# The pair loop of a fused attention and expert kernel written out, and its router steps put at other slots

## The reference, cut to what matters

```python
x = x + tanh(g_xattn) * xattn(layernorm(x), ctx, Wq, Wkv, Wfc, fc_b, qn_w, kn_w)   # 4 heads of 64
x = x + tanh(g_ffn) * ffn(layernorm(x), Wr, We)                                    # 8 experts, top 2

# xattn: q and k are RMS-normalised for each head
attn = softmax(einsum("bqhd,bkhd->bhqk", q, k) * 64 ** -0.5)
out = einsum("bhqk,bkhd->bqhd", attn, v) @ Wfc + fc_b

# ffn: the router
logits = einsum("btd,ed->bte", x, Wr)
top_vals, top_idx = top_k(logits, 2)
w = softmax(top_vals)
pos = cumsum(onehot(top_idx)) - onehot(top_idx)     # place of the token in its expert's queue
keep = pos < 97                                     # capacity of an expert in a batch
out = sum over the two experts e of a token:  w_e * (x @ We[e]) where keep, else 0
```

## Time and profile before

| what | value |
|---|---|
| median of 3 runs | 1496.6 us (1494.82 to 1496.76) |
| span of the profiled execution | 1506.5 us |
| busy share of the span: PE, DVE, ACT, POOL | 95%, 73%, 59%, 51% |
| PE busy, matmuls | 1433.3 us, 8320 |
| granted TensorE clock, mean | 0.983 |
| DMA | 28 GB/s, q14 instruction 81 packets |

### The profile page before, as it was taken

The page is one execution under the profiler, slowest core; times in us unless marked ns, Lnnn a source line. Parts: engine busy times, 40 slices in busy tenths (PEclk is TensorE's granted clock), DMA queues, the critical chain, the costliest instruction groups (busy, mean ns, idle before and its releaser), DMA issues. The chain is left out here.

```text
span 1506.5 us, 30216 instructions
## 1 busy us (share of the span) xinstructions
PE 1433.3 (95%) x8320; PEld 1194.0 (79%) x8320; DVE 1093.6 (73%) x3085; ACT 888.2 (59%) x2536; POOL 764.2 (51%) x915
## 2 busy tenths in 40 slices
PE   5899999999999999999999999999999999999998
PEld 4688887878788887887878878787888878878886
DVE  5667767777777677767778777777776777677763
ACT  6546656656566556566556566565566566666552
POOL 3335455445455445555545555444655554554454
PEclk8689999999999999999999999999999999999999
DMA  4000000000000000000000000000000000000000
GB/s 142 19 1 33 33 31 10 32 26 32 33 15 25 33 25 33 32 10 30 25 33 32 33 7 32 26 32 33 32 7 33 25 33 32 22 18 32 8 16 27
DMA packets 29021, 42.76 MB, mean 28 GB/s; under 512 B 4672, under 2 KB 12288, under 8 KB 28928
## 3 DMA queue, kind: packets, MB, share of 16 engines
q1 hardware_dynamic: 28928, 41.90, 8.1%
HBM read 25.11 MB, written 16.78 MB: 28 GB/s over the span
## 5 line engine op out<-in xcount | busy, mean ns | idle before, releaser
L305 PE MATMUL bkM<-we,x2T 128*128 128x512 f32 x3072 | 789.8, 399 | 1.1 <-DVE acc_v L933 1.1
L305 PEld LDWEIGHTS bkM<-we,x2T 128*128 128x128 f32 x3072 | 556.0, 189 | 110.6 <-DVE acc_v L933 1.8
L606 ACT ACTIVATE a_out<-bkM,gate 128x256 f32<-128x256 f32 x512 | 215.2, 475 | 187.4 <-PE bkM L305 185.1
L450 POOL TENSOR_TENSOR a_sum<-a_sum,a_out 128x256 f32<-128x256 f32 x256 | 188.4, 736 | 131.4 <-ACT a_out L606 112.7
L933 DVE SCALAR_TENSOR_TENSOR acc_v<-bkM,gate,acc_v 128x256 f32<-128x256 f32 x384 | 185.6, 483 | 36.8 <-PE bkM L305 27.0
L406 POOL TENSOR_TENSOR rstd<-ve,minus_half 128x4 f32<-128x4 f32 x64 | 64.8, 1012 | 256.6 <-DVE ve L740 256.6
L406 POOL TENSOR_TENSOR q_r<-q_ve,minus_half 128x16 f32<-128x16 f32 x32 | 93.2, 2911 | 135.0 <-DVE q_ve L816 135.0
L517 ACT ACTIVATE xn<-x_sb,shift,rstd 128x256 f32<-128x256 f32 x128 | 66.5, 590 | 111.8 <-DVE shift L749 111.8
L437 POOL TENSOR_TENSOR probs<-probs,p_inv 128x308 f32<-128x308 f32 x128 | 90.3, 716 | 79.1 <-DVE p_inv L831 79.1
L406 POOL TENSOR_TENSOR k_r<-k_ve,minus_half 77x8 f32<-77x8 f32 x32 | 52.3, 1633 | 122.1 <-DVE k_ve L789 122.1
L455 POOL TENSOR_TENSOR y<-a_sum,acc_v 128x256 f32<-128x256 f32 x128 | 94.0, 735 | 10.9
(11 more groups left out here) (162 smaller groups left out, 2799.1 us busy)
## 6 DMA issues: line engine op xcount, KB each, us to landing
x_sb<-in_x SPq DMA_DIRECT2D x32, 512.0 KB, 3.6
out<-y SPq DMA_DIRECT2D x64, 256.0 KB, 2.0
ctx_sb<-in_ctx SPq DMA_DIRECT2D x32, 154.0 KB
stage<-in_L_ffn_We SPq DMA_DIRECT2D x2, 1024.0 KB, 8.0
stage<-in_L_xattn_Wkv SPq DMA_DIRECT2D x1, 512.0 KB, 5.9
stage<-in_L_xattn_Wq SPq DMA_DIRECT2D x1, 256.0 KB, 6.2
stage<-in_L_xattn_Wfc SPq DMA_DIRECT2D x1, 256.0 KB, 4.1
bias_bc<-in_L_xattn_fc_b SPq DMA_DIRECT2D x1, 128.0 KB, 5.3
```

The source lines that it names most:

```text
L305: mm = nc.tensor.matmul(out, l, r, start=(i == 0), stop=(i == len(terms) - 1))
L450: nc.gpsimd.tensor_tensor(a, o[:, 0] if i == 1 else a, o[:, i], ALU.add).then_inc(a_summed.sem, 1)
L606: ins = nc.scalar.activation(a_out[:, t % 2, (e // 4) * 2 + i], bkM[1][:, i * D:(i + 1) * D], ACT.Copy, scale=gate[:, m.parity, t, e:e + 1])
```

## The change

The hardware loop goes: each engine's program is all 32 rounds in a row, with constant counts in its waits. Inside a round, these steps stand elsewhere:

```diff
-        LOOPS = (PAIRS - 4) // 2
...
+            def pair(n):
+                return Pair(0, n) if n < PAIRS else None
+
             fill()
-            step(Pair(0, 0), Pair(0, 1), Pair(0, 2), Pair(0, 3))
-            with engine.Fori(0, LOOPS) as j:
-                step(Pair(j, 1), Pair(j, 2), Pair(j, 3), Pair(j, 4))
-                step(Pair(j, 2), Pair(j, 3), Pair(j, 4), Pair(j, 5))
-            step(Pair(LOOPS, 1), Pair(LOOPS, 2), Pair(LOOPS, 3), None)
-            step(Pair(LOOPS, 2), Pair(LOOPS, 3), None, None)
-            step(Pair(LOOPS, 3), None, None, None)
+            for n in range(PAIRS):
+                step(pair(n), pair(n + 1), pair(n + 2), pair(n + 3))
```

ScalarE's slots (the move of `x2T_part` ahead of `q(f, 1)` in slot 7 is left out):

```diff
-                if k == 8 and f:
-                    k_part(f)
+                if k == 8:
+                    if f:
+                        k_part(f)
+                    if p:
+                        logits(p)
                 if k == 9:
-                    if p:
-                        logits(p)
                     if f:
                         exps(f, 0)
...
-                if k == 12 and f:
-                    exps(f, 3)
+                if k == 12:
+                    if f:
+                        exps(f, 3)
+                    if p:
+                        router_exp(p)
                 if k == 13:
                     if f:
                         pT_part(f, 0)
                         pT_part(f, 1)
-                    if p:
-                        router_exp(p)
```

VectorE's slots (here too `x2T_part` now stands ahead of `q(f, 1)` in slot 7):

```diff
-                if k == 9 and f:
-                    row_max(f, 0)
-                    row_max(f, 1)
-                    row_max(f, 2)
-                    row_max(f, 3)
-                if k == 10 and m:
-                    experts(m, k)
+                if k == 9:
+                    if f:
+                        row_max(f, 0)
+                    if p:
+                        route(p, 0)
+                    if f:
+                        row_max(f, 1)
+                        row_max(f, 2)
+                        inverse(f, 0)
+                if k == 10:
+                    if m:
+                        experts(m, k)
+                    if f:
+                        row_max(f, 3)
+                        inverse(f, 1)
                 if k == 11:
-                    if f:
-                        inverse(f, 0)
-                    if p:
-                        route(p, 0)
-                    if f:
-                        inverse(f, 1)
+                    if p:
+                        route(p, 1)
+                    if f:
                         inverse(f, 2)
                 if k == 12:
                     if m:
                         experts(m, k)
                     if f:
                         inverse(f, 3)
-                    if p:
-                        route(p, 1)
                 if k == 13 and f:
                     pT_part(f, 0)
                     pT_part(f, 1)
                 if k == 14:
+                    if p:
+                        gates(p)
                     if f:
                         pT_part(f, 2)
                         pT_part(f, 3)
-                    if p:
-                        gates(p)
                     if m:
                         experts(m, k)
```

More of the change, by code:

```diff
@@ L637, in slot @@
                         q(f, 0)
-                        q(f, 1)
                     if p:
@@ L641, in slot @@
                         x2T_part(p, 1)
+                    if f:
+                        q(f, 1)
                     if m:
                         experts(m, k)
-                if k == 8 and f:
-                    k_part(f)
-                if k == 9:
+                if k == 8:
+                    if f:
+                        k_part(f)
                     if p:
                         logits(p)
+                if k == 9:
                     if f:
@@ L987, in slot @@
                         experts(m, k)
-                if k == 9 and f:
-                    row_max(f, 0)
-                    row_max(f, 1)
-                    row_max(f, 2)
-                    row_max(f, 3)
-                if k == 10 and m:
-                    experts(m, k)
-                if k == 11:
+                if k == 9:
                     if f:
-                        inverse(f, 0)
+                        row_max(f, 0)
                     if p:
@@ L1000, in slot @@
                     if f:
+                        row_max(f, 1)
[6 more added lines that the diff above has]
+                        row_max(f, 3)
                         inverse(f, 1)
+                if k == 11:
+                    if p:
+                        route(p, 1)
+                    if f:
                         inverse(f, 2)
@@ L1199, in slot @@
                     kv(f, 1)
-                if k == 5 and f:
-                    q(f, 0)
-                if k == 6:
+                if k == 5:
                     if f:
-                        q(f, 1)
+                        q(f, 0)
                     if p:
@@ L1207, in slot @@
                         x2_transpose(p, 1)
[L1208 to L1211, removed]
+                if k == 6 and f:
+                    q(f, 1)
+                if k == 7:
+                    if f:
+                        q_squares(f)
+                        k_transpose(f)
                     if p:
                         logits(p)
+                if k == 8:
                     if f:
                         scores(f, 0)
+                    if p:
+                        logits_transpose(p)
                 if k == 9 and f:
@@ L1219, in slot @@
                     scores(f, 3)
[L1220 to L1227, removed]
+                if k == 13:
                     if p:
@@ L1230, in slot @@
                     if f:
-                        attend(f, 0, 0, p)
+                        p_transpose(f, 0)
+                        p_transpose(f, 1)
+                        p_transpose(f, 2)
+                        p_transpose(f, 3)
+                if k == 14 and f:
+                    attend(f, 0, 0, p)
                 if k == 15 and f:
```

## The result

| kernel | median of its runs | ratio to before, 95% interval |
|---|---|---|
| before | 1496.27 us (1494.82 to 1496.76) | |
| changed | 1480.22 us (1477.74 to 1481.4) | 0.9891 [0.9877, 0.9905] |

A forecast was written before the change was run, and what follows sets the result against it. PE, busy 1433.3 of 1506.5 us, was taken as the bound, so gains come from its idle time or round length. Span 1506.5 - 16.4 (loop) + 6 (router slots) = 1496.1, less 9.9 gives 1486 us; range 1468 to 1510.

The forecast's parts named there:

- The loop, -16.4 us: VectorE behind the branch back: 13 rounds lose their excess of 1.26 us once the loop is written out, -16.4 us.
- The baseline: Starting time: the traced span of 1506.5 us, taken to stand 9.9 us above the median of the runs.
- The gain at `attend(f, 0, 0)`, 0.5 us left of 1.3: End of a round on PE: low parts come sooner, `attend` starts at 488.2, not 488.72; 0.5 us of 1.3 left.
- the price of `route(p, 0)`: Ahead of tile 1's row maximum: GpSimd holds VectorE's steps, so `exps(f, 1)` starts 1.0 or 1.5 us late; 1.0 taken.
- the forecast's chain: `route(p, 0)` held by GpSimd, `exps(f, 1)` late, `a_out` late, PE's third product waiting, transposes at 485.15, not 484.08.
- `gates`, back to +0.2 us: Before the last two low parts: GpSimd holds `gates`; `attend(f, 0, 1)` from 0.15 us gained to 0.53 lost, +0.2 taken.
- The sum: Whole kernel: 1506.5 - 16.4 + 6 = 1496.1 us of span, less 9.9, rounded to 1486 us.
- the far rival: Router steps: GpSimd hardly blocks them, the tail comes 1.1 to 1.4 us earlier a round, 1438 to 1447 us; chance 0.12.
- The hidden moves: `x2_transpose` one slot earlier, `logits` with its copy and transposes: no cost; a stall of at most 1.1 us at `x2_transpose`.

The follow-up runs named there:

- e1_straight_only: The kernel before with its loop written out on all engines and every step at its old slot: 1478.11 us, ratio 0.9909.
- after_again: The changed kernel, unaltered, measured again on another chip beside the kernel before: 1480.57 us, ratio 0.9935.
- e4_dve_straight: The kernel before with the loop written out on VectorE alone, the other four engines keeping it: 1475.09 us, ratio 0.9888.

## Why the prediction was right, step by step

*The loop, -16.4 us.* Right in place and mechanism, and about right in size. Writing out the loop gave 13.8 us (and 1491.33 - 1476.03 = 15.3 us on the other chip), VectorE alone 16.8; the stall is that of 13 branches on VectorE. The longer straight program shows no stall: VectorE's longest `issue` wait in the changed kernel is 0.4 us. Where the Trainium skill (Runtime: NRT & Kernel Launch, section Instruction fetch mechanics) has sequential blocks fetched ahead and a branch out of the window fetched on demand, these runs agree, with none in the straight program and about 1.2 us of a round for each branch on VectorE; that PE or ScalarE stalls too is not seen. One reading was wrong without harm: the round from 1360.49 to 1405.49 is not a written-out one. The first round behind a branch begins at 221.15, so the 28 rounds of the loop run from 131.28 to 1405.49, and of the two rounds named only the first, 44.90 us, was written out.

*The baseline.* It had two faults that the prediction did not see. It took the trace for a timed execution with 9.9 us around it, and the trace has a round 0.5 us longer than the straight program with the old slots. And it started from 1496.6 us, where the kernel before later stood at 1491.3 to 1491.9. The whole miss of 6 us hangs on this start: from 1491.33 the same working gives 1491.33 - 16.4 + 6 = 1480.9 us, and the changed kernel took 1480.57 on that chip.

*The gain at `attend(f, 0, 0)`, 0.5 us left of 1.3.* The room itself was read too large: the wait there is 1.03 us a round in the trace of before, but 0.72 us in `e1_straight_only`. The length without that wait was read in two ways: 3.35 us from the transposes to `positions`, which includes PE's standing for `both`, and 3.05 us further down; the changed kernel shows 967.63 - 964.45 = 3.18. The wait itself went wholly. The step that failed is the price of `route(p, 0)`: "`exps(f, 1)` starts ... 1.0 or 1.5 us late" and PE's third product waits for `a_out`. In the changed kernel ScalarE was ready at about 958.6 and started at 958.76, 0.2 us late, and PE did not wait. The prediction had read the meeting with GpSimd from a trace of the loop, where the gap between GpSimd's sums is 0.08 us and a sum starts ahead of VectorE's step; written out it is 0.14, and `rank` starts level with the sum. With the loop kept, the forecast's chain came out about as reckoned.

*`gates`, back to +0.2 us.* Right in mechanism: `w_top` and `g_all` are held (0.63 us each), and tile 3's low part makes the second `attend` late. The size was too small. The wait comes to 0.69 us a round, where 2.52 us between the two `attend` had been reckoned and 2.93 came out. Removing it gave 20 to 21 us.

*The sum.* Too high a price at `route(p, 0)` and too low a one at `gates` nearly cancelled: +6 us forecast for the slots, +4.5 measured. So the sum is right by luck in its second half, where two errors of opposite sign offset each other, and the 6 us that are missing between 1486 and 1480 us come from the baseline. The mechanism named for the far rival, that "the router does slip through", is what happened at the first place, by a hundredth of a microsecond; only it didn't pay, because the second place took it back.

*The hidden moves* stayed hidden: no wait on `x2_transpose` or the logits in PE's list is above 1 us.

## What to carry to other kernels

Measure the parts of a change apart: here the half that looked like the point cost 2 to 4.5 us, and one of its moves undone gave 21 us. Before moving small two-operand VectorE steps, look at what GpSimd does at the new place and which of the two starts first; a step of 0.19 us can become 0.6 to 0.8, and that matters where an in-order engine has something urgent behind it. Compare the traced execution's time with the untraced ones before reading hundredths from it.

## What the runs showed of the hardware that was not expected

- Only the engine with the stall needs its loop written out. The other four written out, VectorE not: ratio 1.0007. VectorE alone: 0.9888, against 0.9909 and 0.9898 for all five.
- A VectorE step with two operands in SBUF that starts 6 ns or more after GpSimd's sum is held until the sum ends: `both` in the two traces of the kernel before, 0.78 us, and one `rank` in `after_again`, 0.77 us. One that starts no more than 5 ns after it takes 0.19 us: `both` in `e4_dve_straight` and `rank` in the changed kernel. The sum beside it then takes 0.78 to 0.80 us instead of 0.73.
- The traced execution can differ from the timed ones: the kernel before takes 1508.53 us traced and 1489.91 to 1492.64 untraced, while the straight kernels stay within 4 us. Whether tracing does it, or being the first execution, is open.
- The same router slots cost 2 to 4.5 us in a straight program and 31 us in a loop. One part is that GpSimd's successive sums stand 0.14 us apart in the one and 0.08 in the other. Another is the clock: after 0.76 and 1.30 us of PE idling near the end of a round a five-microsecond stretch had a granted clock of 0.66.
